# A second layer moved ahead of the router products, in place of identity products, in two mixtures of experts of a four-block decoder

## The reference

```python
def _L2_ffn_ref(x, ...):                        # "bit"
    h = (x - mu) / jnp.sqrt(var + LN_EPS) * ln_gamma + ln_beta
    shared_out = jax.nn.silu(jnp.einsum('btd,fd->btf', h, sw1)) @ sw2.T
    probs = jax.nn.softmax(h @ router_w.T, axis=-1)
    top_prob, top_idx = jnp.max(probs, axis=-1), jnp.argmax(probs, axis=-1)
    h1 = jax.nn.silu(jnp.einsum('btd,efd->ebtf', h, ew1))
    eo = jnp.einsum('ebtf,edf->ebtd', h1, ew2)
    gate = jax.nn.one_hot(top_idx, N_EXPERTS) * top_prob[..., None]
    return shared_out + jnp.einsum('ebtd,bte->btd', eo, gate)
```

```python
def _L3_ffn_ref(x, Wg, bg, W1, b1, W2, b2):     # "gate"
    probs = jax.nn.sigmoid(x_flat @ Wg + bg)
    weights = probs * (probs > 0.5)
    h = jax.nn.relu(jnp.einsum('td,edh->eth', x_flat, W1) + b1[:, None, :])
    expert_out = jnp.einsum('eth,ehd->etd', h, W2) + b2[:, None, :]
    return jnp.einsum('te,etd->td', weights, expert_out)
```

## Time and profile before

| | us |
|---|---|
| three executions | 955.29, 959.29, 968.45 (median 959.29) |
| profiled execution, its own time | 955.26 |
| its span in the profile | 953.4 |
| busy: TensorE products | 885.2 (93% of the span) |
| busy: TensorE weight loads | 673.3 (71%) |
| busy: VectorE | 679.5 (71%) |
| busy: ScalarE | 542.3 (57%) |
| busy: GpSimd | 333.1 (35%) |
| DMA | 30.75 MB, mean 32 GB/s |

### The profile page before, as it was taken

How to read it: one execution, slowest core, us unless ns; L and a number is a source line. 1 busy time by engine, 2 the same in 40 slices (tenths; PEclk the granted TensorE clock), 3 DMA queues, 4 the chain that set the end, 5 groups by cost and what they waited for, 6 DMA issues and landing times.

```text
span 953.4 us, 16558 instructions
## 1 busy us (share of the span) xinstructions
PE 885.2 (93%) x6180; PEld 673.3 (71%) x6180; DVE 679.5 (71%) x1318; ACT 542.3 (57%) x1228; POOL 333.1 (35%) x432
## 2 busy tenths in 40 slices
PE   7998999999989899999888789899989998999998
PEld 5556889985576598885444447677879885678787
DVE  6887743558868857865799995776777478854784
ACT  1765434437634567764777773444555557734774
POOL 4862189955326400001288983000000036420000
PEclk9999999999999999999999999999999999999999
DMA  6610011100001004303000001000000000000420
GB/s 127 193 48 13 1 45 45 34 23 2 2 1 46 12 2 126 108 1 132 1 0 1 0 1 45 1 1 2 1 1 2 1 2 1 1 13 23 134 78 23
DMA packets 35202, 30.75 MB, mean 32 GB/s; under 512 B 3948, under 2 KB 28848, under 8 KB 34867
## 3 DMA queue, kind: packets, MB, share of 16 engines
q1 hardware_dynamic: 35123, 29.70, 10.7%
HBM read 29.10 MB, written 0.59 MB: 31 GB/s over the span
## 4 chain that ended last, share of the span: by engine, by line
PE 68%; DVE 14%; POOL 7%; ACT 5%; issue 4%; DMA 0%; POOLq 0%; SPq 0%; DVEq 0%; ACTq 0%
PE banks L951 15%; PE banks L976 14%; POOL work L1804 4%; PE banks L373 4%; PE banks L364 3%; PE banks L1597 3%; DVE work L543 2%; PE banks L1967 2%; PE banks L991 2%; PE banks L990 2%; PE banks L995 2%; PE banks L396 2%; DVE work L535 2%; ACT work L2165 2%; PE banks L1978 2%
## 5 line engine op out<-in xcount | busy, mean ns | idle before, releaser
L1059 ACT ACTIVATE work<-banks,keep 128x512 f32<-128x512 f32 x236 | 157.1, 688 | 126.5 <-PE banks L951 126.4
L951 PE MATMUL banks<-rounded 128*128 128x512 f32 x672 | 169.7, 398 | 2.0 <-ACT work L1059 1.1
L976 PE MATMUL banks<-keep,work 128*128 128x128 f32 x1248 | 148.6, 275 | 0.6 <-ACT work L1059 0.6
L976 PEld LDWEIGHTS banks<-keep,work 128*128 128x128 f32 x1248 | 146.2, 192 | 4.0 <-ACT work L1059 0.7
L951 PEld LDWEIGHTS banks<-rounded 128*128 128x128 f32 x672 | 122.3, 188 | 30.0 <-issue 3.7
L709 ACT ACTIVATE work<-banks,work 128x128 f32<-128x128 f32 (+1 forms) x448 | 121.4, 389 | 29.6 <-DVE work L535 28.5
L150 POOL TENSOR_TENSOR keep<-keep 128x4 f32<-128x4 f32 x26 | 26.8, 1029 | 223.0 <-DVE keep L129 193.1
L1214 DVE SCALAR_TENSOR_TENSOR keep<-banks,keep 128x128 f32<-128x128 f32 x176 | 49.7, 343 | 68.9 <-PE banks L976 68.1
L1804 POOL TENSOR_TENSOR work<-work,keep 128x1024 f32<-128x1024 f32 x31 | 73.1, 2375 | 44.4 <-DVE work L1737 34.8
L535 DVE TENSOR_REDUCE work<-banks 128x8 f32<-128x1024 f32 (+1 forms) x64 | 68.8, 1077 | 26.0 <-PE banks L364 24.7
L1597 PE MATMUL banks<-work,keep 128*128 128x512 f32 x128 | 61.7, 606 | 13.5 <-POOL work L1804 11.9
(11 more groups left out here) (327 smaller groups left out, 1681.2 us busy)
## 6 DMA issues: line engine op xcount, KB each, us to landing
keep<-in_L_ffn_w_dram SPq DMA_DIRECT2D x32, 256.0 KB, 3.5
keep<-in_L_ffn_W_dram SPq DMA_DIRECT2D x16, 256.0 KB, 4.2
shared<-gelu_gate_rows SPq DMA_DIRECT2D x10, 256.0 KB, 3.8
shared<-gate_gate_rows SPq DMA_DIRECT2D x10, 256.0 KB, 3.7
shared<-in_L_xattn_Wkv_dram SPq DMA_DIRECT2D x1, 2048.0 KB, 8.3
shared<-in_L_ffn_expert_w_dram SPq DMA_DIRECT2D x8, 128.0 KB, 2.5
shared<-in_L_ffn_expert_w_dram SPq DMA_DIRECT2D x1, 1024.0 KB, 7.3
keep<-in_L_attn_conv_w_dram SPq DMA_DIRECT2D x1, 1024.0 KB, 7.0
```

The source lines that it names most:

```text
L951: m = pe.matmul(k.ps[:, c, :], w[:, c * P:(c + 1) * P], x[:, h * HALF:(h + 1) * HALF], start=j == 0, stop=j == len(parts) - 1)
L976: m = pe.matmul(k.ps[:, self.bank(n, j), j * P:(j + 1) * P], self.hT[n % 2][:, c, j * P:(j + 1) * P], w2[c], start=c == 0 and self.kind != ...
L1059: act.activation(self.hT[n % 2][:, c, :], k.ps[:, c, :], self.func, bias=bias, scale=scale)\
```

## The change

In the two mixtures `layer2` of the current item (3 in "bit", 1 in "gate") is called right behind the transposes of the second half, ahead of the router products and of `layer1` of the next item. The identity products there are gone, and the call in its old place is left out for that item.

```diff
         for n in range(self.items):
             if n == self.second_at:
                 self.turn.tensor_half(pe, 1)
+                if self.kind in ("bit", "gate"):
+                    self.layer2(pe, n)
                 if self.kind == "bit":
-                    spin(k, pe, 6, 5)
                     self.route_logits(pe, 1)
                 elif self.routed:
                     self.route_logits(pe, 0)
-                if self.kind == "gate":
-                    spin(k, pe, PT0 + 1, 4)
                 if self.kind == "gelu":
                     self.route_logits(pe, 1)
...
             if self.crosses(n):
                 self.layer2_across(pe, n)
-            elif self.kind != "dense":
+            elif self.kind != "dense" and not (self.kind in ("bit", "gate") and n == self.second_at):
                 self.layer2(pe, n)
```

## The result

The changed kernel takes 954.4 us (median of 22 executions, 951.79 to 977.75), the kernel before 957.74 us (median of 22, 955.04 to 968.45). The medians differ by 0.35%. The ratio is 0.9949, with a 95% interval of 0.9929 to 0.9969; it leaves out four executions of the changed kernel as slow (966.49 to 977.75 us) but keeps the one of 968.45 us of the kernel before, and so shows more than the medians do. The forecast was 952.9 us, in a range of 950.8 to 958.8. That range also holds the 955.26 us of an unchanged kernel, so the time alone tests little of the prediction. The distances in the trace test it.

The account below looks back on a forecast made before the run. The prediction took PE to bound the kernel, with 68% of the span's chain of waits. Gains of 1.51 us in "bit" and 0.82 in "gate" sum to 2.33: 955.26 − 2.33 = 952.9 us, range 950.8 to 958.8.

Parts of the forecast that it names:

- "bit", step 1: In "bit", layer2(3) takes the identity products' place; router products start at 733.82, layer1(4) at 734.79 instead of 734.25.
- "bit", step 2: In "bit", layer1(5) waits for ACT behind layer1(4); layer2(4) starts at 737.29 instead of 737.78, gaining 0.49 us.
- "bit", steps 3 and 4: In "bit", add(3) follows add(2), the ranks end 2.01 us earlier, ACT itself is late, hidden(6) starts 1.51 earlier.
- "bit", step 5: In "bit", layer1(7) waits for ACT until 742.21 instead of 743.72; gain 1.51 us, PE's stall about 0.25.
- "gate", step 1: In "gate", layer2(1) starts where the router products stood, hiding the wait for the split; layer1(3) gains 1.19 us.
- "gate", step 2: In "gate", second router products come 2.38 us later, layer2(2) waits for add(0); gain falls from 1.19 to 0.82.
- "gate", step 3: In "gate", the split of expert 2's weights ends at 873.45 instead of 871.73, with 1.39 us to spare before layer1(4).
- "only gate": The chain at hidden(6) in "bit" isn't shortened, only "gate" gains 0.82 us: 954.4 us; chance 12%.
- The table switch: On ACT in "bit", a switch costs up to 1.00 us beyond its load, leaving 1.33 us gain: 953.9 us; chance 4%.
- The full gains: Shorter delay at layer1(5) in "bit" and route in time in "gate": 2.01 + 1.19 = 3.20 us, 952.1 us; chance 12%.

Follow-up runs that it names:

- three more moves: Changed kernel with "gate" second router products ahead of layer1(2), "bit" router products behind layer1(4), "gate" exponentials ahead of hidden(2): ratio 0.9967, span 949.2 us.
- the kernel with both router moves: Changed kernel with second router products ahead of layer1(2) in "gate" and router products behind layer1(4) in "bit": ratio 0.9963, span 950.2 us.

## Why the prediction was right

The sum was 2.33 us, and the marks of the trace show 1.73 + 0.94 = 2.67, the spans 2.8. The share between the places was right as well: 1.51 and 0.82 forecast. Both terms came out too small, by 0.22 and 0.12 us, so the sum isn't right by errors that cancel. By its own steps:

- "bit", step 1: `layer1(4)` came 2.68 us behind the first mark, not 2.87. From `layer2(3)` to the router products it took 1.79 instead of the 1.90 of a row further on, and the router products 0.89 instead of 0.97. This 0.19 us is nearly all of the term's miss, as each later start hangs on it. The trace of before has the 1.79 in a row where `layer2` stands right behind transposes, as it does after the change; the row taken stands behind a `layer1`:

```profile
769.55 1.87 PEld L976 LDWEIGHTS banks<-keep,work 128*128 128x128 f32 x16
771.34 0.77 PEld L951 LDWEIGHTS banks<-rounded 128*128 128x128 f32 x4
```

- "bit", step 2: `hidden(4)` came 0.83 behind, forecast 0.84. From there `layer1(5)` 0.80, `hidden(5)` 1.64 and `layer2(4)` 1.66; forecast 0.81, 1.64 and 1.66. The pattern taken from `hidden(6)` held to 0.01 us.
- "bit", steps 3 and 4: `add(3)` follows `add(2)`, the ranks end 0.25 us before ACT takes them (forecast 0.5), and ACT is last: `hidden(6)` comes 9.27 us behind the first mark, forecast 9.48. (The prediction's own terms add up to 741.38 for it, not 741.40.)
- "bit", step 5: PE's stall is 0.21, forecast 0.25. The run with the router products later agrees with ACT as the last engine: with `layer1(4)` earlier, `layer1(7)` came earlier.
- "gate", step 1: 3.57, 0.89, 2.62 and 1.00 us, forecast 3.57, 1.01, 2.63 and 1.01. Again the router products behind a `layer2` took 0.12 less.
- "gate", step 2: `add(0)` came 3.07 us behind the second router products, as forecast, and held `layer2(2)`, with 0.39 given back (forecast 0.37).
- "gate", step 3: the split of expert 2's weights ended at 885.58, 1.34 us ahead of `layer1(4)`; forecast 1.39.
- The identity products cost nothing where they stood: shown in "bit" by spans at full clock, and in "gate" by the trace (12.26 and 12.27 us), since no execution without them there had full clock from start to end. What the prediction doesn't say is how much hangs on removing them once `layer2` stands in their place: with them left in the gain is 0.65 us.

The rivals: "only gate" fell with the run that had the change in "bit" alone. The table switch has no cost beyond its load: 751.07 + 1.28, and the exponentials follow at 752.36 with no wait for DVE to hide anything. The drain that the Trainium skill gives for every switch (ScalarE: Activation LUTs, What ACT_TABLE_LOAD costs) is in no row of this case. (With it at both switches the prediction's sum would be 955.7, not 955.6 us.) The clock was full in both places in the profile of the changed kernel.

One test that the prediction set itself was badly put: it would be wrong if the granted clock were under 1.00 anywhere. It was, from 300 to 340 us, but the kernel before again shows the same, so this fall isn't evidence against the change's mechanism. It was so once more between 810 and 820 us (0.83 in these 10 us), between the two changed places, where neither profile of the kernel before has it. No run shows what brought that one, and the marks don't contain it. The full gains (3.20 us) were not out of reach: three more moves bring 3.20 by the marks.

What stays open: the spans at full clock show 0.1 to 0.6 us more than the marks in all kernels with the move in "bit" but the one with the identity products put back, and most in the kernel with "bit" alone (2.3 against 1.73) and in the last one with ACT's exponentials early (3.8 against 3.20). Between the profile of before and that of the kernel with both router moves, both at full clock, 0.52 us of the 3.2 are there ahead of both places, at the transposes of "bit" (731.48 and 730.96), and behind the marks the offset grows by no more than 0.07. So the excess probably lies in the start of the program, or in the scatter of a few executions; no run separates the two.

## What to carry to other kernels

Work of the same queue that has all its inputs is a better filler for a wait than products that nobody reads. In "bit" it also let a chain on other engines go, the addition and the ranks behind `layer2(3)`. But the old filler has to leave when the work comes in: it was free under the wait, and it cost 2.02 us of the 2.67 when it stood behind the moved work. Ask of the move what becomes late by it; the answer was ACT's table load in "bit" and the gate weights in "gate", and a consumer is only helped if every engine on the way to it has its turn earlier, as the exponentials behind `hidden(2)` showed. A pattern of waits taken from another place of the same trace, as that behind `hidden(6)`, predicted a new wait here to a few hundredths of a us. The length of a step is best taken from a row with the same neighbour ahead of it: a `layer2` took 1.79 us behind transposes and 1.90 behind a `layer1`.

## What the runs showed of the hardware

The granted clock of a single core falls to 1.2 GHz for stretches in most executions of the same program, and only some 15% of them (17 of 117 of before, and the one of 1754.3 us) have a mean clock of 1.000. From 300 to 340 us, in self attention, it stayed at 0.50 although PE was busy for 40.00 of 40.00 us, in some executions of both kernels. These are the first 10 us of it in the changed kernel, and the same 10 us of the kernel before:

```profile
300.00:310.00 10.00, 10.00 (x66) 6.13 (x64) 4.68 (x10) 4.09 (x15) 4.73 (x12) 0.50 0.00 0
300.00:310.00 10.00, 9.55 (x104) 5.99 (x102) 7.26 (x16) 5.52 (x20) 7.82 (x20) 1.00 0.01 2
```

The Trainium skill has it that "the default state is throttled, and activity releases the throttle" (TensorE: Matmul & The Clock Gate, What's actually happening). In these rows PE and its weight loads are busy for no less of the time at half clock (10.00 and 6.13 us) than at full clock (9.55 and 5.99), and in the 10 us ahead the two kernels have nearly the same work (9.18 and 6.97 us, 9.15 and 6.77). So busy time alone doesn't tell the two apart, and what brings the low clock is open.

Such a stretch is what makes up the 13 us by which some executions are longer: from 16 identity loads ahead of it to the first `layer1` behind it the kernel before takes 37.46 us at full clock (294.53 to 331.99) and 50.78 us at half clock (294.13 to 344.91, in its second profile).
